# Recurrent layer of an eight-stage network: the chains folded by tensor_reduce over three planes, the input half's difference made by GpSimd, the tanh's select by a predicated copy

## The reference, cut to what matters

```python
xw = jnp.einsum('ntd,dh->nth', x, Wx) + b
def step(prev_h, xw_t):
    next_h = jnp.tanh(prev_h @ Wh + xw_t)
    return (next_h, next_h)
_, hs = jax.lax.scan(step, h0, jnp.swapaxes(xw, 0, 1))
```

## Time and profile before

| | us |
|---|---|
| median of 3 runs (8298.24 to 8300.0) | 8299.39 |
| span of the profiled execution | 8311.2 |
| DVE busy, PE busy, ACT busy, POOL busy | 6987.2, 6754.2, 4891.1, 1902.8 |
| recurrent layer, first to last `pre` (128 steps) | 308.7 to 4988.8 |

### The profile page before, as it was taken

How to read it: one execution, slowest core, us unless ns; L and a number is a source line. 1 busy time by engine, 2 the same in 40 slices (tenths; PEclk the granted TensorE clock), 3 DMA queues, 4 the chain that set the end, 5 groups by cost and what they waited for, 6 DMA issues and landing times. The chain is left out here.

```text
span 8311.2 us, 122846 instructions
## 1 busy us (share of the span) xinstructions
PE 6754.2 (81%) x38193; PEld 2748.6 (33%) x38193; DVE 6987.2 (84%) x12707; ACT 4891.1 (59%) x5846; POOL 1902.8 (23%) x1514
## 2 busy tenths in 40 slices
PE   4788888888888888888888883588888888782889
PEld 1233333333333333333333331233333333341553
DVE  4799999999999999999999996899999999446333
ACT  3677777777777777777777772244444444222322
POOL 0000001001001001001000110588788888000000
PEclk8999999999999999999999996799999999996999
DMA  1211111111111111111111110000000000000000
GB/s 37 37 27 32 32 27 32 32 27 32 27 32 32 27 32 30 29 32 28 31 32 27 32 32 24 18 4 3 4 3 3 4 3 3 2 6 3 3 15 5
DMA packets 51335, 174.59 MB, mean 21 GB/s; under 512 B 5857, under 2 KB 13794, under 8 KB 49698
## 3 DMA queue, kind: packets, MB, share of 16 engines
q0 software_dynamic: 37264, 145.91, 9.9%
q1 hardware_dynamic: 13586, 22.47, 1.0%
HBM read 15.12 MB, written 7.34 MB: 3 GB/s over the span
## 5 line engine op out<-in xcount | busy, mean ns | idle before, releaser
L980 POOL TENSOR_TENSOR hc<-hh,cg 128x512 f32<-128x512 f32 x1024 | 1290.4, 1267 | 349.8 <-DVE hh L962 349.5
L902 ACT ACTIVATE ps_m<-ps_m,aneg 128x508 f32<-128x508 f32 x1024 | 674.4, 659 | 1121.2 <-DVE hh L962 1011.2
L962 DVE TENSOR_TENSOR_SCAN hh<-ps_m,bx 128x512 f32<-128x512 f32 x1024 | 1228.7, 1213 | 13.7 <-POOL bx L984 13.7
L476 POOL TENSOR_TENSOR r_gate<-ident 128x1 f32<-128x1 f32 x137 | 213.7, 1560 | 4475.4 <-DVE rx_s L564 4413.3
L327 PE MATMUL r_ps<-wdiag,whq 128*128 128x512 bf16 x4480 | 1057.7, 382 | 216.3 <-DVE rh_gain L189 76.4
L866 PE MATMUL ps_m<-hc,pick 128*128 128x512 f32 x2048 | 1056.9, 600 | 8.0 <-POOL hc L980 6.8
L571 DVE TENSOR_TENSOR_SCAN co<-rx_d 128x772 f32<-128x772 f32 x544 | 924.0, 1761 | 0.0
L571 DVE TENSOR_TENSOR_SCAN co<-rh_d 128x772 f32<-128x772 f32 x512 | 862.5, 1747 | 15.6
L300 PE MATMUL r_ps<-rx_nd,ident 128*128 128x512 f32 x1096 | 557.4, 655 | 200.7 <-DMA rx_nd<-rx_s 200.7
L327 PEld LDWEIGHTS r_ps<-wdiag,whq 128*128 128x128 bf16 x4480 | 395.3, 98 | 836.9 <-issue 139.3
L941 DVE TENSOR_TENSOR bx<-ps_m,bg 128x512 f32<-128x512 f32 x896 | 596.8, 672 | 89.4 <-PE ps_m L882 89.0
(11 more groups left out here) (412 smaller groups left out, 11921.0 us busy)
## 6 DMA issues: line engine op xcount, KB each, us to landing
rx_nd<-rx_s POOLq DMA_DIRECT2D x137, 1040.0 KB, 8.0
rows_scratch<-pc SPq DMA_DIRECT2D x48, 128.0 KB
rows<-rows_scratch SPq DMA_DIRECT2D x128, 48.0 KB
ew<-in_e SPq DMA_DIRECT2D x3, 1024.0 KB, 7.4
co<-in_x_dn SPq DMA_DIRECT2D x1, 1024.0 KB, 4.8
xcur<-in_x_dn SPq DMA_DIRECT2D x1, 1024.0 KB
out_x<-xcur SPq DMA_DIRECT2D x1, 1024.0 KB, 3.9
qi<-in_f_q SPq DMA_DIRECT2D x1, 384.0 KB, 3.0
```

Source lines behind the costliest of these rows:

```text
L902: e.activation(da[un % NDA][:, :, 1:T], ps[:, un % 2, :].rearrange("p (n t) -> p n t", n=NG4)[:, :, 1:T], ACT.Exp, scale=aneg[:, 0:1]).the ...
L962: e.tensor_tensor_scan(hh[un % NBUF][:], da[un % NDA].rearrange("p n t -> p (n t)"), bx[un % NBUF][:], 0.0, ALU.mult, ALU.add).then_inc(sc ...
L980: e.tensor_tensor(hc[un % NHC][:], hh[un % NBUF][:], cg[:], ALU.mult).then_inc(weighted, 1)
```

## The change

- The interleaved arrays go. Each half has one array `planes` of three planes of 16 x 130: minus the difference (`nd`), the remainder (`rho`) and the sum (`s`), and each producer writes its plane in place. The ACT copies of L391, L394 and L397 go, and the remainder copies become four contiguous ones for R and two for X.
- `chain` is a `tensor_reduce` over (k, c) of a quarter: 4 rows x 128 k x 3 planes, read with c innermost. Neighbouring reads lie 16 x 130 x 4 = 8320 bytes apart.
- X's difference is a GpSimd `tensor_tensor` on 2048 elements instead of a DMA; the gate operation and the negated ACT copy go. In two of eight steps it now stands behind GpSimd's copies.
- DVE's order: the first X chain stands at the head of the step, where the first half of X's prefix stood; the other three stand behind R's difference, and the whole of X's prefix behind them.
- PE's order: X's minus-sums come before the next X product, X's differences and small products behind it. The 28 fillers stay; their gates move with the shorter tanh.
- The tanh has 39 instead of 44 DVE instructions up to h: the absolute value and two of the selecting multiplies and adds go, one `copy_predicated` on 32 elements comes.

The diff, cut to what the text speaks of:

```diff
+            f = dict(pd=sb(tag + "pd", [128, N, K2]), planes=sb(tag + "planes", [128, 3, N, K2]), ends=sb(tag + "ends", [128, N]))
+            f["nd"], f["rho"], f["s"] = (f["planes"][:, c] for c in (MINUS_D, RHO, SUM))
...
-            n_ = tl.inc(e.tensor_scalar(ab[:], pre[:], -1.0, None, ALU.mult))
-            j = tl.inc(e.tensor_tensor(mask[:], ab[:], pre[:], ALU.max))
-            tl.inc(e.tensor_scalar(big[:], mask[:], TANH_SMALL, None, ALU.is_ge))
-            tl.inc(e.scalar_tensor_tensor(out=small[:], in0=mask[:], scalar=TANH_SMALL, in1=cl[:], op0=ALU.is_lt, op1=ALU.mult))
+            tl.inc(e.tensor_scalar(small[:], x2[:], TANH_SMALL_SQUARED, None, ALU.is_lt))
...
-            tl.inc(e.tensor_tensor(rcb[:], rc[:], big[:], ALU.mult))
-            i = tl.inc(e.tensor_tensor(qsel[:], qq[:], big[:], ALU.mult))
-            tl.inc(e.tensor_tensor(qsel[:], qsel[:], small[:], ALU.add))
+            tl.inc(e.copy_predicated(quot[:], raw(small[:]).unsqueeze(1).to_broadcast([128, 2, N]), plain[:]))
+            tl.wait(s_ + 1)
...
-        IN_TANH = ((9, 4), (14, 4), (19, 4), (23, 4), (26, 5), (36, 4), (44, 3))
+        IN_TANH = ((6, 4), (11, 4), (16, 4), (20, 4), (23, 5), (32, 4), (39, 3))
...
                     sticky(4, (ra, KA * t + A_SIGNED))
+                    minus_sums(0, X, (xs, 3 * g + 3))
+                    if s == UN - 2:
+                        e.wait_ge(stp, i + 3)
+                    e.wait_ge(ra, KA * t + A_SIGNED + NRC)
+                    product(4, xp_stat, x_mov((s + 2) % UN)).then_inc(xp_mm, 1)
                     if s == UN - 1:
                         e.wait_ge(stl, i + 3)
-                    remainder(0, X, xl_stat, x_mov((s + 1) % UN), (xs, 3 * g + 3), (xd, 16 * (g + 1)), x_diff, True).then_inc(xl_mm, 1)
-                    if s == UN - 2:
-                        e.wait_ge(stp, i + 3)
-                    e.wait_ge(ra, KA * t + A_PUT + 2 * NRC)
-                    product(4, xp_stat, x_mov((s + 2) % UN)).then_inc(xp_mm, 1)
-                    e.wait_ge(xa, 5 * g + 5)
+                    remainder(0, X, xl_stat, x_mov((s + 1) % UN), (xd, g + 1), True).then_inc(xl_mm, 1)
+                    e.wait_ge(xa, KXA * g + 3)
...
+            def put_remainders(F, bank0, n, done):
+                e.activation(F["rho"][:, n, 2:K2].rearrange("p n (b k) -> p n b k", k=KB),
+                             ps[:, bank0:bank0 + NB, :].rearrange("p b (n k) -> p n b k", n=N)[:, n], ACT.Copy).then_inc(done, 1)
...
-                    put_sums_of(R, 0, ra)
-                    e.wait_ge(v, KV * t + V0 + V_DIFF)
-                    put_differences(R, R["gain"][:], ra)
                     e.wait_ge(re_mm, t + 1)
                     for c in range(NRC):
-                        for odd in range(2):
-                            put_remainders(R, 4, quarter(c), odd, ra)
-                    e.wait_ge(xc, KXC * g)
-                    parts(g, 0)
+                        put_remainders(R, 4, quarter(c), ra)
...
-                    e.wait_ge(xa, 5 * g + 5)
-                    e.wait_ge(xp_mm, g + 2)
-                    copy_out(X, 4, xa)
-                    copy_negative(xn)
+                    x_remainders(g)
+                    x_products(g + 1)
...
             def x_difference(g):
-                e.wait_ge(xn, g + 1)
+                e.wait_ge(xc, KXC * g)
                 e.wait_ge(xs, 3 * g + 3)
-                e.wait_ge(xg, g + 1)
-                e.tensor_tensor(gate[:, 2:3], ident[:, 0:1], ident[:, 1:2], ALU.add).then_inc(xg, 1)
-                e.dma_start(flat(X["nd"][:]), flat(X["s"][:]), accum_op=ALU.add, max_dma_last_dim=4 * N * K2 // 2).then_inc(xd, 16)
+                e.tensor_tensor(X["nd"][:, :, 2:K2], X["pd"][:, :, 2:K2], X["s"][:, :, 2:K2], ALU.subtract).then_inc(xd, 1)
...
-                return e.tensor_tensor_scan(co[:, at], F["d"][:, 0, 1:][:, at], F["d"][:, 1, 0:N * LX][:, at], 0.0, ALU.add, ALU.add)
+            def chain(F, n):
+                return e.tensor_reduce(F["ends"][:, n], F["planes"][:, :, n, 2:K2].rearrange("p c n k -> p n k c"), XY, ALU.add)
...
-                    x_prefix_odd(g, HALVES[0])
+                    x_chain_first(g - 1)
...
-                    tl.inc(difference(R["gain"][:], R))
-                    x_prefix_odd(g, HALVES[1])
-                    x_prefix_even(g)
-                    x_chain(g - 1, s)
-                    e.wait_ge(xc, KXC * g)
+                    tl.inc(difference(R))
+                    x_chain_rest(g - 1, s)
+                    x_prefix(g)
```

More of the change, by code:

```diff
@@ L117, in rnn @@
         V0 = 1
-        VSETUP = 60
+        VSETUP = 55
         class Tally:
@@ L290, in residue, with minus_sums @@
                 return ins
-            def remainder(bank0, F, stat, mov, prefixed, differenced, diff, last, own=NB, seeded=None):
+            def minus_sums(bank0, F, prefixed, own=NB):
                 e.wait_ge(*prefixed)
@@ L295, in remainder @@
                     e.matmul(ps[:, bank0 + b, :], negid[:], piece(F, "s", b), start=True, stop=False)
+            def remainder(bank0, F, stat, mov, differenced, last, own=NB, seeded=None):
                 e.wait_ge(*differenced)
@@ L564, in prefix_even @@
                 return e.tensor_tensor(F["s"][:, :, 2:K2:2], F["s"][:, :, 1:D:2], F["pd"][:, :, 2:K2:2], ALU.add)
-            def difference(out, F):
-                return e.tensor_tensor(out, F["s"][:, :, 2:K2], F["pd"][:, :, 2:K2], ALU.subtract)
-            def chain(F, lo, hi_):
-                at = slice(lo * LX, hi_ * LX)
-                return e.tensor_tensor_scan(co[:, at], F["d"][:, 0, 1:][:, at], F["d"][:, 1, 0:N * LX][:, at], 0.0, ALU.add, ALU.add)
-            def x_prefix_odd(g, part, later=True):
-                e.wait_ge(xa, 5 * g + 1)
-                if later:
-                    e.wait_ge(xd, 16 * g)
-                prefix_odd(X, part).then_inc(xs, 1)
@@ L579, in x_prefix_even, with difference, x_prefix @@
-            def x_prefix_even(g):
+            def difference(F):
+                return e.tensor_tensor(F["nd"][:, :, 2:K2], F["pd"][:, :, 2:K2], F["s"][:, :, 2:K2], ALU.subtract)
+            def chain(F, n):
+                return e.tensor_reduce(F["ends"][:, n], F["planes"][:, :, n, 2:K2].rearrange("p c n k -> p n k c"), XY, ALU.add)
+            def x_prefix(g):
+                e.wait_ge(xa, KXA * g + 1)
+                for part in HALVES:
+                    prefix_odd(X, part).then_inc(xs, 1)
@@ L580, in x_prefix_even, with x_chain_first, x_chain_rest @@
                 e.wait_ge(xs, 3 * g + 2)
                 prefix_even(X).then_inc(xs, 1)
-            def x_chain(g, u):
-                e.wait_ge(xa, 5 * g + 5)
-                tx = Tally(e, xc, KXC * g)
-                for c in range(NXC):
-                    tx.inc(chain(X, c * N // NXC, (c + 1) * N // NXC))
+            def x_chain_first(g):
+                e.wait_ge(xa, KXA * g + 2)
+                chain(X, quarter(0)).then_inc(xc, 1)
+            def x_chain_rest(g, u):
+                tx = Tally(e, xc, KXC * g + 1)
+                e.wait_ge(xa, KXA * g + 3)
+                for c in range(1, NXC):
+                    tx.inc(chain(X, quarter(c)))
@@ L588, in x_chain @@
                 tx.wait(tx.n)
-                tx.inc(e.tensor_tensor(xwt[:, N * u:N * (u + 1)], ends, brow[:, N * u:N * (u + 1)], ALU.add))
+                tx.inc(e.tensor_tensor(xwt[:, N * u:N * (u + 1)], X["ends"][:], brow[:, N * u:N * (u + 1)], ALU.add))
             for g in range(AHEAD):
-                for part in HALVES:
-                    x_prefix_odd(g, part, g > 0)
-                x_prefix_even(g)
                 if g:
-                    x_chain(g - 1, g - 1)
+                    x_chain_first(g - 1)
+                    x_chain_rest(g - 1, g - 1)
@@ L620, in _ @@
                         e.wait_ge(xw_cp, i + 1)
-                    j = tl.inc(e.tensor_tensor(pre[:], ends, xwT[:, s, :], ALU.add))
+                    j = tl.inc(e.tensor_tensor(pre[:], R["ends"][:], xwT[:, s, :], ALU.add))
                     j = tanh(tl, e, j, (tri, 3 * t + 3))
```

143 lines of the change are left out of this document (52 added, 91 removed).

## The result

| us | before | after |
|---|---|---|
| median of the runs | 8299.15 (8298.24 to 8300.0) | 8409.47 (8404.32 to 8411.71) |
| span of the profiled execution | 8311.2 | 8409.9 |
| recurrent layer, first to last `pre` | 308.7 to 4988.8 | 278.9 to 5078.2 |
| median spacing of two `pre`, turns of the loop left out | 36.12 | 36.99 |

The ratio of the times is 1.0134 (95% interval 1.0121 to 1.0146): 110 us slower. The forecast was 946 us slower. The profiled execution of before was a slow one of its kind (span 8311.2 beside a median of 8299.15), so the two spans lie only 99 us apart, and the layer of before in the profile may be some 12 us longer than in its median execution.

What follows compares the result with a forecast made beforehand. DVE, with 1.0 us to spare, was taken to bound the step. +6.90 us a step over 128 steps (+883), clock +50 and prologue +13 gave +946 on the median 8299.4: 9245 us, range 8260 to 9480.

Steps and rivals of the forecast that it cites:

- third rival: PE's queue: folds at contiguous price (1.75 us), fillers delay `h_product`; 36.4 us a step, 8307 in all; chance 0.21.
- The chains: DVE's quarter folds: each `tensor_reduce` taken at 2.71 us, with ends 1.75 and 3.22; a chain takes 0.97 us more.
- R's chains: R's four folds on DVE, each 0.97 us longer: +3.87 us a step.
- the other two: DVE's head of the step (one X chain, +0.99 us) and middle (three X chains and whole X prefix, +2.19 us).
- The tanh: From `pre` to h, 5 DVE instructions fewer: -0.15 us a step taken, bounds 0 and -0.85.
- GpSimd's difference: X's difference on GpSimd, 2048 elements: 4.8 to 5.1 us, taken as not held by the reduces beside it.
- the gate's 1.57 us: GpSimd's one-element gate operation before the change took 1.57 us, seemingly held by a two-input X scan on DVE.
- GpSimd's column copies: Copies ahead of GpSimd's X difference in two of eight steps, lying in GpSimd's idle time: forecast to cost nothing.
- clock term: Granted clock falling after PE's 4.0 us idle ahead of X's minus-sums: up to +0.75 us a step, 0.4 taken, +50.
- the likeliest case: The forecast's own case: folds at 2.71 us, DVE sets the step, 9245 us, own range 9080 to 9480; chance 0.47.
- The prologue: Nine groups ahead of the recurrent layer, 27.8 us each instead of 26.5: +13 us, or -12 with contiguous folds.
- What would show it: Listed signs: reduce 2.7 or 1.75 us; R's prefix 3.7 or 2.7, first R chain 21 or 17.4 us behind `h_product`.

Runs made afterwards that it cites:

- experiment 1: 32 reduces of 1536 elements in different layouts added behind the changed kernel's last layer: contiguous 1.75 us, three planes 0.16 us more, four planes 2.74 us.
- Experiment 7: The kernel before with only the new tanh (selection by predicated copy, filler places moved with it): 8295.83 us, ratio 0.9999.
- experiment 6: The kernel before with X's difference made by one GpSimd sum instead of the accumulating DMA, chains still two-input scans: 8793.17 us, ratio 1.0603.
- experiment 5: The changed kernel with seven more filler matmuls on PE between R's last products and X's minus-sums: 8400.32 us, ratio 1.0127.

## Why the prediction was wrong

The direction came right by luck: "slower" was forecast because the folds would be dear and DVE would set the step. The folds were cheap, and the kernel is slower because `h_product` waits for PE's fillers, its third rival, which it gave a chance of 0.21 and, of that, 0.08 for a slower kernel.

- **The chains** failed. The bound 1.75 was nearer than the value taken: measured 1.91, so 0.16 a chain over contiguous and not 0.96; the slowdown of 110 us is far from the 883 that this term gave. The step that failed is "I take 2.71, the same instruction with the same kind of pattern". L1516 walks through eight places before it comes back, L223 through two, the change through three. The two rows were read as a clean one and a thin one; experiment 1 fits both, each for its own count. By the earlier trace rows the rate of eight places is 1.67 ns; experiment 1 has 1.68 at four planes and 1.76 to 1.78 from six on. This one term carried 0.99 + 2.19 + 3.87 of the 6.90 us a step; R's chains cost 0.64 (forecast 3.87), and the other two went below nothing together (-0.35).
- **The rule of the Trainium skill** ("SBUF — State Buffer", Specifications) that a read crossing into a new 16-byte line pays would have every read of the fold pay. Experiment 1 bears it out from four planes on and not for two; for three, a sixth of the earlier trace rows's 0.625 ns is there.
- **The tanh** was mis-sized: -0.24 by the medians of all steps (-0.44 in the step shown) against -0.15, within its bounds. Experiment 7 shows that alone it gives nothing that the times can tell from no change.
- **GpSimd's difference** held: not held up by the folds, 4.55 us against 4.8 to 5.1. The suspicion that the gate's 1.57 us was such a hold is borne out by experiment 6, which shows scan and GpSimd holding each other. GpSimd's column copies cost nothing, as forecast. What the forecast left out is that the DMA that it replaces comes late in a quarter of before's steps; that going is worth about 30 us.
- **Rival 3** had the mechanism. It gave X's copies until C + 12.9, fillers until C + 19.0 and 36.4 a step; the timeline has the copies' end at 2438.83 = C + 12.98 and H at C + 19.09. Its 8307 missed by 102 us: the fold at 1.91 instead of 1.75 and the handovers put C at H + 17.72, not 17.4, and the steps with slow fillers were not in it. It should have had the clock term that the likeliest case had.
- **The clock term** was put to the 4.0 us ahead of X's minus-sums. With cheap folds that idle time is 1.67 us, and filling it changed nothing (experiment 5); the clock falls behind the 2.1 to 2.2 us ahead of the fillers, a place that the forecast did not name. Against before it costs about 36 us by the estimate above, where 50 were set: near in size, for another reason.
- **The prologue**: -30 against +13 (or -12 with contiguous folds). One group of it takes 23.9 us instead of 26.2 (from one group's first X chain to the next's), against 27.8 forecast; with GpSimd's sum alone (experiment 6) it is 25.2. The rest was not taken apart.
- **What would show it**: R's prefix stands 2.58 behind H and the first R chain 17.72, close to the third case's 2.7 and 17.4. Of "DVE idle over 1 us ahead of R's prefix" only 0.35 came, since `h_product` starts late.

## What to carry to other kernels

Price a strided operand by how many places the read visits before it comes back to a neighbour of the first, not by its stride alone, and measure it when the nearest rows stand on both sides. Before a GpSimd operation is put beside DVE work, count that work's inputs from SBUF. And when work leaves DVE or the order changes, look at what else stands in PE's queue ahead of the critical matmul: matmuls that only keep the clock up cost time as soon as they start late. Last, before an average is put down to one cause, look at the long steps one by one: here both kernels had them, for different reasons.

## What the runs showed of the hardware that was not expected

- The step between three and four planes: 1.90 us against 2.74 for 1536 elements, with two planes at the contiguous price and 6 to 16 planes at 2.86 to 2.88, and the distance of the planes (2080 or 8320 bytes) without effect at three.
- A DVE scan with two inputs and a GpSimd sum exclude each other for whole instructions (6.07 and 5.89 us instead of 1.74 and 4.55). GpSimd's column copies take 2.02 us each in the kernel before, where they stand beside these scans, and 0.50 in the kernel after, where they stand beside folds or small tanh instructions.
- The granted clock fell behind 2.2 us of idle PE ahead of the fillers in 42 of after's 127 steps and not in the others of the same make; behind before's 1.86 us at the same place it never fell.
- The difference DMA of the kernel before kept PE waiting 1.0 us in most steps and 2.2 to 2.4 in 30 of 119.
